# f_tail moved to the head of the loop, and a per-half wait for the transposes of xq2

## The reference, cut to what matters

```python
x = x + _layernorm(attn(_layernorm(x), W_qkv, W_o))        # linear attention, chunks of 64
x = x + _layernorm(ffn(_layernorm(x), w1, b1, w2, b2, gamma, beta))

def ffn(x, w1, b1, w2, b2, gamma, beta):
    h = layernorm(x, gamma, beta)
    h = qlinear(h, w1, b1)                 # 1024 -> 4096
    h = jax.nn.gelu(h, approximate=False)
    return qlinear(h, w2, b2)              # 4096 -> 1024

def qlinear(x, w, b):
    xq, sx = act_quant(x)     # scale 127 / max|x| of each token, rounded
    wq, sw = weight_quant(w)  # rounded to -1, 0, 1
    return xq @ wq.T / (sx * sw) + b
```

## Time and profile before

| | us |
|---|---|
| median of 3 runs | 3528.62 (3527.16 to 3531.42) |
| profiled execution | 3528.98 |
| its span, slowest core (6) | 3527.4 |
| spans of the 8 cores | 3480.7 to 3527.4 |
| TensorE matmul busy | 2107.8 (60%) |
| VectorE busy | 1538.8 (44%) |
| ScalarE busy | 724.1 (21%) |
| mean granted TensorE clock, core 6 | 0.775 of full speed |

### The profile page before, as it was taken

How to read it: one execution, slowest core, us unless ns; L and a number is a source line. 1 busy time by engine, 2 the same in 40 slices (tenths; PEclk the granted TensorE clock), 3 DMA queues, 4 the chain that set the end, 5 groups by cost and what they waited for, 6 DMA issues and landing times.

```text
span 3527.4 us, 33827 instructions; the slowest of 8 cores (3480.7 to 3527.4 us)
## 1 busy us (share of the span) xinstructions
PE 2107.8 (60%) x10604; PEld 1038.5 (29%) x10640; DVE 1538.8 (44%) x2492; ACT 724.1 (21%) x1193; POOL 147.7 (4%) x203
## 2 busy tenths in 40 slices
PE   0061566747766367647776376747686366657665
PEld 0040444412222144312222143413232244313222
DVE  0575544345553143445452234355452244355542
ACT  0030322112221121212221112122221122122221
POOL 0141300000000000000000000000000000000000
PEclk9999676768888667668888667668888676678887
DMA  9797901131221310131121311131112311031111
GB/s 189 248 193 243 190 20 35 25 104 27 42 42 32 130 31 25 28 113 32 26 42 39 125 28 26 26 113 36 30 33 39 128 26 33 18 117 33 42 31 41
DMA packets 333137, 245.50 MB, mean 70 GB/s; under 512 B 304272, under 2 KB 304288, under 8 KB 328864
## 3 DMA queue, kind: packets, MB, share of 16 engines
q0 software_dynamic: 97440, 184.58, 19.3%
q1 hardware_dynamic: 235520, 58.74, 9.1%
HBM read 159.41 MB, written 33.55 MB: 55 GB/s over the span
## 4 chain that ended last, share of the span: by engine, by line
PE 42%; DMA 21%; DVE 19%; ACT 8%; issue 7%; DVEq 1%; another core or an unknown queue 0%; SPq 0%; ACTq 0%; POOLq 0%; POOL 0%; PEldq 0%; PEld 0%
PE pb L988 14%; PE pb L906 13%; DMA abf<-abf 6%; PE pb L492 6%; DMA af<-x 5%; DMA af<-w 4%; PE pb L499 3%; DMA w2q_t<-w2qs 3%; PE pb L909 2%; DMA out<-x 1%; DMA wqkv_t<-w_qkv 1%; DVE abf L576 1%; DVE af L569 1%; ACT af L1029 1%; DVE x L1034 1%
## 5 line engine op out<-in xcount | busy, mean ns | idle before, releaser
L906 PE MATMUL pb<-w1q_t,abf 128*128 128x512 fp8e4 x2048 | 541.6, 412 | 391.4 <-DMA abf<-abf 332.2
L988 PE MATMUL pb<-w2q_t,abf 128*128 128x512 fp8e4 x2048 | 500.6, 407 | 77.7 <-ACT s2rowr L977 44.3
L906 PEld LDWEIGHTS pb<-w1q_t,abf 128*128 128x128 bf16 x2048 | 190.7, 103 | 668.6 <-issue 512.9
L492 PE MATMUL pb<-abf,wqkv_t 128*128 128x128 bf16 x2048 | 195.4, 287 | 257.8 <-DMA abf<-abf 257.8
L988 PEld LDWEIGHTS pb<-w2q_t,abf 128*128 128x128 bf16 x2048 | 207.3, 103 | 353.3 <-issue 154.3
L492 PEld LDWEIGHTS pb<-abf,wqkv_t 128*128 128x128 bf16 x2048 | 190.8, 135 | 261.7 <-issue 261.7
L921 DVE TENSOR_REDUCE khs<-af 128x1 f32<-128x1024 f32 x128 | 156.1, 1220 | 179.1 <-ACT af L917 115.2
L1021 DVE RECIPROCAL scal<-scal 128x1 f32<-128x1 f32 x32 | 5.2, 164 | 474.8 <-ACT scal L1017 474.8
L528 DVE TENSOR_REDUCE khs<-pb 128x8 f32<-128x512 f32 x32 | 22.1, 691 | 434.2 <-ACT af L509 434.2
L917 ACT ACTIVATE af<-pb,scal 128x512 f32<-128x512 f32 x256 | 161.4, 684 | 228.6 <-PE pb L909 228.0
L1001 ACT ACTIVATE af<-pb,scal 128x512 f32<-128x512 f32 x32 | 22.0, 687 | 561.8 <-PE pb L992 561.8
(11 more groups left out here) (162 smaller groups left out, 2753.8 us busy)
## 6 DMA issues: line engine op xcount, KB each, us to landing
af<-w POOLq DMA_DIRECT2D x16, 2048.0 KB, 9.9
wqkv_t<-qkvs POOLq DMA_DIRECT2D x3, 6144.0 KB, 24.3
af<-w POOLq DMA_DIRECT2D x32, 512.0 KB, 5.4
af<-w POOLq DMA_DIRECT2D x16, 1024.0 KB, 8.8
af<-x POOLq DMA_DIRECT2D x32, 512.0 KB, 3.8
w1q_t<-w1qs POOLq DMA_DIRECT2D x4, 4096.0 KB, 16.1
w2q_t<-w2qs POOLq DMA_DIRECT2D x4, 4096.0 KB, 27.0
out<-x POOLq DMA_DIRECT2D x32, 512.0 KB, 2.9
```

The costliest lines, as they stand in the source:

```text
L492: mi = PE.matmul(pq, lhsT=wqkv[:, kk, m * 128:(m + 1) * 128], rhs=hf[:, kk, :], start=(kk == 0), stop=(kk == 7))
L906: PE.matmul(Bk[bb0 + n2][:, :], lhsT=xf[:, kk, :], rhs=w1q[:, kk, hs0:hs0 + 512], start=(kk == 0), stop=False)
L988: mi = PE.matmul(Bk[4 + n2][:, :], lhsT=xq2_fm[:, kk, :], rhs=w2q[:, kk, n2 * 512:n2 * 512 + 512], start=(kk == 0), stop=False)
```

## The change

There are two edits in the feed-forward part. f_tail(gg-1) moves from the end of iteration gg to its beginning, before the transpose of tile gg+1 and f_q2(gg); the tail of the last tile still follows the loop. And SyncE's wait ahead of the transposes of xq2 now asks, for each half, for the end of the same half of the previous tile's f2. Before, half 0 waited for the end of the whole previous f2, and half 1 had no wait of its own. No instruction that computes is added or removed.

```diff
@@ -958,8 +958,8 @@
                     half = hh // 2
                     ms[f"dv_xq2b_{seg}_{gg}_{half}"] = cnt["dv"]
                     SY.wait_ge(s_dv, cnt["dv"])
-                    if gg >= 1 and half == 0:
-                        SY.wait_ge(s_pe, ms[f"pe_f2_{seg}_{gg-1}_1"])
+                    if gg >= 1:
+                        SY.wait_ge(s_pe, ms[f"pe_f2_{seg}_{gg-1}_{half}"])
                     tp_dma(xq2_fm[:, half * 16:half * 16 + 16, :],
                            xq2_tm[:, half * 2048:(half + 1) * 2048])
                     ms[f"tp_xq2_{seg}_{gg}_{half}"] = cnt["tp"]
@@ -1044,6 +1044,8 @@
             f_front(1)
         f_f1(0)
         for gg in range(G):
+            if gg >= 1:
+                f_tail(gg - 1)
             if gg + 1 < G:
                 f_front_tp(gg + 1)
             f_q2(gg)
@@ -1052,8 +1054,6 @@
             if gg + 1 < G:
                 f_f1(gg + 1)
             f_f2(gg)
-            if gg >= 1:
-                f_tail(gg - 1)
         f_tail(G - 1)
         ms[f"pe_ffn_done_{seg}"] = cnt["pe"]
```

## The result

The changed kernel takes 3601.29 us (median of 8 runs, 3598.47 to 3607.45) where the kernel before takes 3527.89 us (8 runs). The ratio is 1.0215, 95% interval 1.0201 to 1.0230: slower by 73 us. The forecast was 3600 us. All medians and ratios here leave out executions in a slower state, in which the cores of a die show a lower granted clock than usual and need more time. The profiled execution took 3607.45 us with a span of 3605.9 us on core 6, 78.5 us over the span before; it was the slowest of the eight. In the mean of the eight cores the spans of the two profiled executions differ by 81.4 us (3508.4 and 3589.8).

A forecast was written before the change was run, and what follows sets the result against it. TensorE was taken to idle ahead of f1 on f_tail's chain, behind the newest f2's eviction. Terms 64.8 + 39.0 + 7.8 - 14.0 gave +97.6 us, less 25 from the clock: 3529 became 3601, rounded to 3600 us, range 3564 to 3630.

The forecast's parts named there:

- What bounded the kernel before: Feed-forward stage: TensorE stands still 13.6 us ahead of f1, all hanging on f_tail, whose square root queues behind f2(gg)'s eviction.
- The stats on the path: In f_tail, bn_stats and aggregate can start only after the newest f2's eviction: 1.95 us more in each gap.
- The table load behind its wait: In f_tail, ScalarE's table load follows the stats; rival, it runs ahead of its wait: 36 us less, 3565 us, chance 0.08.
- One gap more in each segment: Between f2(0) and f1(2), tail(0), its store and the transpose now stand: 16.2 us more per segment.
- One tail fewer at the end: After f2(7) only tail 7 follows, so its stats start sooner: 3.5 us less per segment.
- The loosened wait: SyncE's per-half wait ahead of the xq2 transposes is over long before q2's data are there: price and gain 0.
- The clock: TensorE's f2 and f1: half of 24 dips gone, 20 us, and f1 0.2 us shorter, 5 us, given back.
- the other side: Rival: the tail doesn't hold f1 back, no gap grows, only segment ends change: 3515 us, faster by 0.4%, chance 0.03.

The follow-up runs named there:

- tail_mid: Changed kernel with f_tail(gg-1) emitted inside f_f2(gg), between the scale-row copy and the eviction of z(gg): 3164.5 us, ratio 0.8977 to the kernel before.

## Why the prediction was right

*What bounded the kernel before* was read rightly: the tail's ScalarE work stood behind the eviction of the newest f2, although its data were a tile old. tail_mid shows it by the opposite: with that order undone, and nothing computed less, the gap of 13.7 us is down to the pause of 1.8.

*The stats on the path.* Predicted 1.95 us a gap, measured 2.01. The doubled stats show the switch: 1.54 us more of them cost 0.02 us a gap in the order before, and 1.52 us in the order after.

*The table load behind its wait.* In the chain after the change it begins 0.11 us after the aggregate. The earlier place that the Trainium skill leaves open (ScalarE activation tables: per-element evaluation and per-set limits, Table sets in the compiler and the runtime) wasn't used; the trace agrees with the forecast's choice from the earlier trace rows.

*One gap more in each segment.* Predicted 16.2 us, measured 16.37; with tail 0 a tile later it is gone (35.52 us from f2(0) to f2(1)). It is the largest term: 4 x 16.37 = 65 us.

*One tail fewer at the end.* Predicted 3.5 us, and the distance from eviction to stats fell by 3.50 (3.61 to 0.11). The whole rest between two stages is shorter by 4.8 us; the other 1.3 us are within its scatter, for in the eight traces of kernels in which one tail follows f2(7) and its stats aren't doubled the rest is 374.9 to 378.5 us.

*The loosened wait.* Price 0, measured 0.9987 with an interval over 1. It is worth something only where q2's data are there before f2 ends.

*The clock.* Half of the dips were taken as gone, 20 us; 86 of 172 went, 24 x 0.75 = 18 us. f1 didn't become shorter by 0.2 us but longer by 0.11, so the 5 us of that half of the term were wrong in sign; f2(7), which I had left out, became shorter by 0.79 us, 3 us in all. The two errors cancel in part: 18 - 2 + 3 = 19 us given back instead of 25. The prediction had read the regularity on core 6 (23 of 24); over all cores it was 172 of 192, a little less.

That longer intervals would end the repetition was right, and the traces show it: before the change a dip was followed by a dip in the next tile in 120 of 140 cases, after it in 8 of 67. That the share would be a half was a choice, not a derivation. It could have come out otherwise: with 1.5 us more in the gap (the doubled stats) a dip is again followed by a dip in 89 of 120 cases, and 152 of 192 f2 had it. There the size of this term was luck.

The sum by measured terms: 65.5 + 20 x 2.01 + 4 x 2.08 - 4 x 3.5 - 19 = 81 us. These terms are means over all cores, and the mean of the eight spans rose by 81.4 us. The slowest core rose by 78.5 us, the medians by 73.4. The forecast's sum was 97.6 - 25 = 72.6 us. That it meets the medians within 1 us is luck too: against the means, which its terms describe, it is 9 us short, 6 of them in what the clock gives back.

*Where the reasoning fell short* is a rival. I gave the other side (the transpose isn't held back by the store) as 3515 us. The run with the transpose first made exactly that condition true, f1 started 1.7 us behind f2, and the time was 3604 us. I had priced the removal of a wait without asking what is due next; a third slab that waited 0.90 us for a GELU was the sign of it, in the trace of the changed kernel. It could be seen in the trace before as well (timeline of core 6, f1(3)):

```profile
897.60 1.26 ACT L917 ACTIVATE af<-pb,scal 128x512 f32<-128x512 f32 x2
```

These GELUs end at 898.86, and the third slab, which needs the banks that they free, starts at 899.26. So the second chain had 0.40 us to spare there, and 0.48 us in the mean of f1(3) to f1(7) of all cores.

## What to carry to other kernels

In queues that run in order, old work can wait for new work merely because of where it is emitted. Look for the operation whose data have long been there and which still waits, and ask what stands ahead of it in the queue of each engine that it uses; then place its steps where those queues are idle, not at the loop's end or head for neatness. Before a wait is removed, follow the second chain to the same point: two chains of equal length gave nothing here until both were shortened.

## What the runs showed of the hardware

The dips of TensorE's clock at the start of f2 don't follow from the length of the pause ahead of it. Pauses of 1.79 to 2.17 us were followed by a dip and pauses of 1.69 to 2.17 us by none.

What decides is the moment. On each core all changes of the granted clock between 1.2 and 2.4 GHz lie on one grid of equal steps through the whole execution, to 0.01 us, in all twelve traces. Sorted by where in such a step it starts, f2 falls into two classes. Of the 2688 f2 of tiles 0 to 6 of all twelve traces, 1410 start beyond a certain place in the step, and 1407 of these had the dip; 1278 start before it, and 2 had it. The five exceptions lie within 0.05 us of the step's end. This was read from the traces of kernels made for other ends, in which starts fall at many places; no run was made to shift the start alone. The Trainium skill (TensorE: Matmul & The Clock Gate, The HAM clock gate) says that the share of half-rate matmuls depends on the moment at which they start; these traces agree.

So the interval of a loop sets the number of dips by whether it brings the next f2 to the same place of the grid. Of 192 f2 172 were hit at an interval of 51.2 us, 86 at 52.6 and 152 at 54.5. The same edit can be worth some 3 us more or less in a stage by this alone.
